# Second attention of a four-layer kernel: the largest-score pass in two row tiles, key preparation on GpSimd, the causal mask partly added by TensorE

## The reference, cut to what matters

```python
def _L1_attn_ref(x, w_attn, w_proj):      # B 8, T 512, D 128, H 16, HEAD_D 8
    qkv = x @ w_attn
    q = qkv[..., :D].reshape(Bv, Tv, H, HEAD_D).transpose(0, 2, 1, 3)
    k = qkv[..., D:D + HEAD_D]
    v = qkv[..., D + HEAD_D:]
    att = jnp.einsum('bhqd,bkd->bhqk', q, k) * scale
    att = jnp.where(causal[None, None, :, :], att, -jnp.inf)
    att = jax.nn.softmax(att, axis=-1)
    y = jnp.einsum('bhqk,bkd->bhqd', att, v)
    ...
    return y @ w_proj
x = x + _L1_attn_ref(_layernorm(x), L1_attn_w_attn, L1_attn_w_proj)
```

## Time and profile before

| what | us |
|---|---|
| median of 3 runs (848.96 to 860.17) | 853.83 |
| the profiled execution | 861.02 |
| its span, first to last instruction | 859.3 |
| third layer's largest-score pass of sequence 0, before turn 0 | 470 to 504 |
| one steady turn (four of them alike) | 41.60 |

### The profile page before, as it was taken

The page is one execution under the profiler, slowest core; times in us unless marked ns, Lnnn a source line. Parts: engine busy times, 40 slices in busy tenths (PEclk is TensorE's granted clock), DMA queues, the critical chain, the costliest instruction groups (busy, mean ns, idle before and its releaser), DMA issues. The chain is left out here.

```text
span 859.3 us, 14978 instructions
## 1 busy us (share of the span) xinstructions
PE 681.4 (79%) x4376; PEld 413.4 (48%) x4409; DVE 583.3 (68%) x1923; ACT 349.4 (41%) x748; POOL 328.8 (38%) x430
## 2 busy tenths in 40 slices
PE   1579989984048999999974779898989898898794
PEld 1445666652025788777762224444444444443353
DVE  8378888886921312544357988888889898977373
ACT  0322333304302212222311127666666666666761
POOL 0256656640065636677630003333333332333330
PEclk9999999997558859999995579999999999999996
DMA  9200000000411212222234213020404040300021
GB/s 297 80 1 1 0 1 0 1 1 26 134 40 32 37 19 35 34 40 38 35 77 55 37 22 49 12 57 3 56 4 56 3 57 9 50 4 3 1 62 38
DMA packets 40350, 32.44 MB, mean 38 GB/s; under 512 B 3608, under 2 KB 36936, under 8 KB 40280
## 3 DMA queue, kind: packets, MB, share of 16 engines
q1 hardware_dynamic: 30448, 23.51, 12.6%
q0 software_dynamic: 7840, 6.86, 5.4%
q10 hardware_dynamic: 1992, 1.21, 0.8%
HBM read 13.60 MB, written 8.13 MB: 25 GB/s over the span
## 5 line engine op out<-in xcount | busy, mean ns | idle before, releaser
L1602 ACT ACTIVATE pexp<-wide 128x512 f32<-128x512 f32 (+2 forms) x384 | 183.7, 543 | 118.5 <-PE wide L1791 112.3
L1551 POOL TENSOR_SCALAR_AFFINE_SELECT pexp<-pexp 128x256 f32<-128x256 f32 x256 | 107.3, 422 | 284.1 <-ACT pexp L1602 282.6
L1414 DVE CUSTOM_DVE_ANT_0 masked<-bank,mask_qk 128x384 f32<-128x384 f32 (+3 forms) x356 | 155.2, 480 | 22.0 <-PE bank L1742 20.0
L1791 PE MATMUL wide<-qT,kTe 128*128 128x256 bf16 (+3 forms) x501 | 120.7, 301 | 19.0 <-ACT pexp L1602 8.8
L1070 ACT ACTIVATE hT<-wide,b1T 128x512 f32<-128x512 f32 x64 | 43.5, 687 | 162.8 <-PE wide L1090 134.3
L1742 PE MATMUL bank<-kTm,qT 128*128 128x384 bf16 (+3 forms) x348 | 89.0, 320 | 17.1 <-DVE mx L1414 8.7
L1804 PE MATMUL bank<-pexp,vx 128*32 128x512 f32 (+3 forms) x1024 | 95.5, 445 | 0.8 <-POOL pexp L1551 0.8
L945 POOL DMA_INDIRECT x_dram<-yg,row_u x40 | 63.9, 1596 | 58.0 <-DVE yg L994 49.5
L1414 DVE CUSTOM_DVE_ANT_0 masked<-wide,mask_qk 128x256 f32<-128x256 f32 (+3 forms) x156 | 74.3, 499 | 15.5 <-PE wide L1742 12.9
L938 POOL DMA_INDIRECT x_row<-xln_dram,row_u x64 | 61.8, 965 | 52.8 <-DVE slot_tok L815 33.6
L1099 PE MATMUL bank<-w_sb,hT 128*128 128x128 f32 x512 | 75.4, 292 | 3.2 <-issue 3.2
(11 more groups left out here) (232 smaller groups left out, 1071.8 us busy)
## 6 DMA issues: line engine op xcount, KB each, us to landing
qT<-qp SPq DMA_DIRECT2D x135, 64.0 KB
x_sb<-in_L_attn_x SPq DMA_DIRECT2D x8, 256.0 KB, 6.7
w_sb<-in_L_ffn_w SPq DMA_DIRECT2D x1, 2048.0 KB, 13.1
xln_dram<-rx SPq DMA_DIRECT2D x8, 256.0 KB, 2.3
out_x<-x_sb SPq DMA_DIRECT2D x8, 256.0 KB, 2.3
x_dram<-x_sb SPq DMA_DIRECT2D x5, 256.0 KB, 3.5
x_sb<-x_dram SPq DMA_DIRECT2D x5, 256.0 KB, 3.0
x_row<-xln_dram,row_u POOLq DMA_INDIRECT x64
```

The lines of the kernel that those rows point to most:

```text
L1414: ins = nc.vector.tensor_tensor_reduce(out=masked[:, n % 4, at], in0=bank_of(n)[:, at], in1=mask_qk[:, T - w:T], scale=1.0, scalar=LEAST, ...
L1551: nc.gpsimd.affine_select(out=pexp[:, n % 4, :, 0:P], in_=pexp[:, n % 4, :, 0:P], pattern=[[0, 2], [1, P]], compare_op=ALU.is_ge, fill=0.0 ...
L1602: nc.scalar.activation(pexp[:, (2 * step + h // 2) % 4, h % 2:h % 2 + nh, 0:w], psE[m % 3][:, 0:nh * w].rearrange("p (h t) -> p h t", h=nh ...
L1791: ins = nc.tensor.matmul(psE[m % 3][:, hh * w:(hh + 1) * w], kTe[:, par, j * P:(j + 1) * P], qT[:, b % QB, 4 * qd + h + hh, j * P:T], star ...
```

## The change

- **Row tiles.** `qT` and `kTm` get 15 blocks of 8 rows (120) in place of nine (72). Heads 0 to 7 have their six largest products in rows 0 to 47, heads 8 to 15 in rows 64 to 111, and the other three products further down. The largest-score pass now uses those six products alone, so that a unit of heads 0 to 7 and one of heads 8 to 15 form a pair: their matmuls have 48 rows each, in rows 0 to 63 and 64 to 127 of the array, and go to two banks. The second pass goes on with all nine (rows 0 to 122 with the three for the maximum; the blocks of the other half are zero).
- **Pairs.** Units are issued two at a time, so `PAIRS_IN_STEP` takes the place of `IN_STEP`; the pair waits for both banks and for the query rows of both halves.
- **Mask.** For query tiles 0 and 1 PE adds the mask by four more matmuls of 64 rows per pair (identity against mask, own and other half of the rows), and DVE takes the maxima of the whole bank with one `tensor_reduce`. Tiles 2 and 3 stay as they were.
- **Keys on POOL.** The five operations of the key parts, the key slots (four copies in place of three) and the values' copy move from DVE to POOL, into its order before the zeroings of steps 6, 7 and 2. The DVE copy `kTe` is gone: `kTm` has three buffers and the rows of -1, which POOL writes at the program's start after the constants have come.
- **Zeros.** The start clears 64 rows of half the heads twice, instead of `kTm` and 64 rows of all heads. The constants grow by 256 columns, 128 KB.

```diff
-    QR = PARTS * PARTS * L
+    BLOCKS = 2 * P // 16 - 1
+    QR = BLOCKS * L
+    LARGE = 6 * L
+    ROWS_OF_HALF = (((0, 3, 5), (1, 4, 6), (2, 7, 14)), ((8, 11, 13), (9, 12, 6), (10, 7, 14)))
+    KEYS_IN_BLOCKS = ((0, 0, 2, 0, 3), (1, 0, 2, 3, 5), (1, 0, 1, 7, 8), (2, 0, 2, 5, 7))
...
-        IN_STEP = (4, 3, 2, 2, 1, 2, 2, 2, 5, 4, 3, 3, 2, 4, 2, 3)
-        AHEAD = sum(IN_STEP[SHIFT_STEP:])
+        PAIRS_IN_STEP = (2, 2, 1, 1, 1, 1, 1, 0, 2, 2, 2, 1, 1, 1, 2, 2)
+        AHEAD = 2 * sum(PAIRS_IN_STEP[SHIFT_STEP:])
...
+                n = 2 * (spot in spots[:PAIRS_IN_STEP[s]])
...
+            part, g0, ng, lo, hi = KEYS_IN_BLOCKS[n]
+            return ops(kx3[:, :, g0:g0 + ng, lo % 8:lo % 8 + hi - lo, :],
+                       kp[:, part].unsqueeze(2).unsqueeze(2).broadcast_to([P, NT, ng, hi - lo, L]))
...
+        def pool_k_parts(pool, b):
+            pool.wait_ge(q_kv.sem, q_kv.at(b, 1))
+            pool.wait_ge(q_kx.sem, q_kx.at(b, 0))
+            split(pool, nc.gpsimd, q_kpart, b, kv2[:, :, 0:L], k_rest[:, :, :], [kp[:, n] for n in range(PARTS)])
...
-        def dve_kTe(dve, b, par):
...
+                if k in MASKED_BY_PE:
+                    nc.vector.tensor_reduce(mx[:, k, h:h + nh], bank_of(n)[:, :].rearrange("p (h t) -> p h t", h=nh),
+                                            AX.X, ALU.max).then_inc(q_mx.sem, 1)
+                    continue
...
+        def pool_turn(pool, b, middle=True, front=True):
+            for s in range(STEPS):
+                if middle and s == V_STEP:
+                    pool_v(pool, b + 1, 1 - b % 2)
+                if front and s == K_SPLIT_STEP:
+                    pool_k_parts(pool, b + 2)
+                if front and s == SLOT_STEP:
+                    pool_k_slots(pool, b + 2)
+                pool_causal(pool, b, 2 * s)
+                pool_causal(pool, b, 2 * s + 1)
...
-        def pe_max_unit(pe, b, n, place):
+        def pe_max_pair(pe, b, n, places):
+
             k, h, nh = max_units[n]
-            pe.wait_ge(q_row[h // 8].sem, q_row[h // 8].at(b, PARTS * PARTS))
+            for half in range(2):
+                pe.wait_ge(q_row[half].sem, q_row[half].at(b, PARTS * PARTS))
             pe.wait_ge(q_kTm.sem, q_kTm.at(b, 1))
             w = P * (k + 1)
             for hh in range(nh):
-                ins = nc.tensor.matmul(place[:, hh * w:(hh + 1) * w], qT[:, b % QB, h + hh, k * P:(k + 1) * P],
-                                       kTm[:, b % 2, 0:w], start=True, stop=True)
-            ins.then_inc(q_smp.sem, 1)
+                for half, place in enumerate(places):
+                    rows = slice(64 * half, 64 * half + LARGE)
+                    ins = nc.tensor.matmul(place[:, hh * w:(hh + 1) * w],
+                                           qT[rows, b % QB, 8 * half + h + hh, k * P:(k + 1) * P],
+                                           kTm[rows, b % QB, 0:w],
+                                           start=hh == 0 or k not in MASKED_BY_PE, stop=k not in MASKED_BY_PE)
+                    if hh == nh - 1 and k not in MASKED_BY_PE:
+                        ins.then_inc(q_smp.sem, 1)
+            if k in MASKED_BY_PE:
+                for whose in ("own", "other"):
+                    for half, place in enumerate(places):
+                        rows = slice(64 * half, 64 * half + 64)
+                        ins = nc.tensor.matmul(place[:, :].rearrange("p (h t) -> p h t", h=nh)[:, :, w - P:w],
+                                               by_mask["ident_" + whose][rows, :],
+                                               by_mask["causal_" + whose][rows, :].unsqueeze(1).broadcast_to([64, nh, P]),
+                                               start=False, stop=whose == "other")
+                        if whose == "other":
+                            ins.then_inc(q_smp.sem, 1)
...
-            nc.vector.memset(kTm[64:P, :, :], 0.0).then_inc(s_zero.sem, 1)
-            nc.vector.memset(qT[64:P, :, :, :], 0.0).then_inc(s_zero.sem, 1)
+            nc.vector.memset(qT[64:P, :, 0:HEADS // 2, :], 0.0).then_inc(s_zero.sem, 1)
+            nc.vector.memset(qT[0:64, :, HEADS // 2:HEADS, :], 0.0).then_inc(s_zero.sem, 1)
```

More of the change, by code:

```diff
@@ L1367, in split @@
                 if n:
-                    dve.wait_ge(sig.sem, sig.at(b, n))
+                    engine.wait_ge(sig.sem, sig.at(b, n))
                 if n % 2 == 0:
-                    nc.vector.tensor_copy(part, whole if n == 0 else rest).then_inc(sig.sem, 1)
+                    on.tensor_copy(part, whole if n == 0 else rest).then_inc(sig.sem, 1)
                 else:
[L1372 to L1377, removed]
@@ L1395, in dve_kTe, with dve_q_parts @@
-        def dve_kTe(dve, b, par):
[L1396 to L1399, removed]
+                    on.tensor_tensor(rest, whole if n == 1 else rest, part, ALU.subtract).then_inc(sig.sem, 1)
+        def dve_q_parts(dve, b, ops):
+            split(dve, nc.vector, q_qpart, b, psA[:, :], q_rest[:, :], [qp[:, n] for n in range(PARTS)], ops)
@@ L1424, in dve_shift @@
             dve.wait_ge(q_mTp.sem, q_mTp.at(b, 0))
[L1425 removed]
+            split(dve, nc.vector, q_mpart, b, mx[:, :, :], mx[:, :, :], [mp[:, :, n, :] for n in range(PARTS)])
         def dve_shift_T(dve, b):
@@ L1553, in pool_causal @@
                                     channel_multiplier=-1).then_inc(q_pc.sem, 1)
-        def mqa_pool(pool):
-            with nc.gpsimd.Fori(0, B) as b:
-                for n in range(NX):
-                    pool_causal(pool, b, n)
+        def pool_turn(pool, b, middle=True, front=True):
[8 more added lines that the diff above has]
+                pool_causal(pool, b, 2 * s + 1)
+        def mqa_pool(pool):
+            pool_k_parts(pool, 0)
+            pool_k_slots(pool, 0)
+            pool.wait_ge(q_init.sem, q_init.total(4))
+            pool_v(pool, 0, 0)
+            pool_k_parts(pool, 1)
+            pool_k_slots(pool, 1)
+            for b in range(B):
+                pool_turn(pool, b, middle=b + 1 < B, front=b + 2 < B)
         def act_xln(act, b, tiles=range(NT)):
@@ L1680, in q_rows @@
                 queue.wait_ge(q_qpart.sem, q_qpart.at(b, 2 * n + 1))
-                for j in range(PARTS):
-                    row = (n * PARTS + j) * L
+                for block in ROWS_OF_HALF[half][n]:
+                    row = block * L
                     queue.dma_start(qT[row:row + L, b % QB, 8 * half:8 * half + 8, :],
@@ L1986, in constants @@
         "seqmask": ((n[:, None] % 64) // 8) == np.arange(8)[None, :],
-        "shift_rows": np.where((n >= 72) & (n < 75), -1.0, 0.0)[:, None],
+        "shift_rows": np.where((n >= 120) & (n < 123), -1.0, 0.0)[:, None],
     }
+    causal = parts["causal_qk"]
+    for name, a in (("ident_own", np.eye(P)), ("ident_other", np.roll(np.eye(P), P // 2, axis=0)),
+                    ("causal_own", causal), ("causal_other", np.roll(causal, P // 2, axis=0))):
+        halves = np.ascontiguousarray(a, np.float32).view(np.uint32) >> 16
+        parts[name] = (halves[:, 0::2] | (halves[:, 1::2] << 16)).astype(np.uint32).view(np.float32)
     layout, at = {}, 0
```

107 lines of the change are left out of this document (47 added, 60 removed).

## The result

The kernel after took 876.15 us (875.04 to 878.82, four runs), the kernel before 851.81 in the same session: a ratio of 1.0274, 95% interval 1.0194 to 1.0353. Repeated with the experiments, on a chip where the kernel before takes 838 us, it was 865.75 us and 1.0334 (1.0317 to 1.0352). The forecast was 852 us, range 831 to 870: wrong in sign and outside the range.

A forecast was written before the change was run, and what follows sets the result against it. No engine was held full; DVE and PE hand PSUM banks back and forth, each late at times. Turns with POOL -2.9, before turn 0 +1.3, start -0.5: -2.1 from the 853.8 us median gives 852, range 831 to 870.

The forecast's parts named there:

- DVE, maxima and keys: DVE in a turn: 1.5 us saved on maxima, 1.7 on keys, together 3.2 us (2.0 to 3.6).
- PE, streams and shape changes: PE in a turn: 2.6 us of streams saved, 37 shape changes at 0.10 us cost 3.7, net 1.1 us more.
- Rivals 2 and 3: PE in the turns: shape changes make it the bound, 874 to 882, chance 0.14; row tiles don't stream together, 888, 0.04.
- rival 2: PE becomes the bound through 37 shape changes a turn at 0.20 us each; 874 to 882 us, chance 0.14.
- POOL: POOL's key work at steps 6 and 7 delays the values: 0.75 us per turn (0 to 1.5), six turns, +4.5.
- What a turn gains: Steady turn: DVE's -3.2 and PE's +1.1 both halved, -1.05 us; seven turns -7.4, with POOL's +4.5 -2.9.
- Before turn 0: Pass ahead of turn 0: first pair waits for both halves' query rows, 4 us later; together +1.3 us (-1 to +4).
- given back: 3.5: Pass before turn 0: 1.5 us of maxima, 1.4 + 0.6 of sequence 1's keys and DVE's wait for them regained.
- Rival 4: The pass before turn 0 loses more, +4 us with nothing in the turns: 857 us, chance 0.06.
- Turn 0: First of the seven turns' worth of maxima (turns 0 to 6), counted at the same -1.05 us each.
- The program's start: DVE's clearing at the start: same 12288 words, without the 0.48 us for `kTm`; -0.5 us (-3 if the gap was real).
- I am wrong in the middle if the schedule of units ... set the turn: Closing caveat on the turns: which bank comes free when is beyond the engines' sums; no size or chance given.

The follow-up runs named there:

- e2: Kernel after with the turns' key parts, key slots and values' copy back on DVE at their old places; ratio 1.0262 to the kernel before.
- f1: Kernel before with keys and values' copy on POOL behind the zeroings, three key buffers, no `kTe`; single units in old order, mask on DVE; ratio 0.9934.
- e4: Kernel after without row tiles: maxima products over rows 0 to 119, mask products over 128 rows, unit after unit; ratio 1.0262.
- f2: f1 with PE adding the mask of tiles 0 and 1 over the whole array; ratio 0.9971, steady turn 41.4 us.
- h4: Kernel before in spread single units, keys and mask on DVE, with the pairs' numbers per step and without the `kTe` copy; ratio 1.0012.
- f3: Kernel before with the pairs' order, whole array, mask and turns' keys on DVE, start's keys on POOL, three key buffers, no `kTe`; ratio 1.0205.
- g2: f3 with the old numbering, so both units of a pair are of one half; ratio 1.0108.
- h1: g1 with a step's two units spread over places B and D (then A and C) instead of both at B; ratio 1.0121.
- g1: f3 with units issued one by one, each waiting only for its own bank and its own half's rows; ratio 1.0178.
- e1: Kernel after with DVE's divide ahead of the two maxima where a place has both; ratio 1.0247, steady turn 43.1 us.
- e3: Kernel after with POOL's key parts and slots behind the two zeroings of their step instead of ahead; ratio 1.0247.
- h2: f3 with one pair moved from step 1 to step 7 and one from step 14 to step 13; ratio 1.0299.
- h3: Kernel after with the edits of e1 and e3 and the pairs per step of h2; ratio 1.0074.
- i2: Kernel after, unchanged, run again on the chip of the experiments; ratio 1.0334, attention stage 435.4 us.

## Why the prediction was wrong

- **DVE, maxima and keys:** right in sum, 33.16 busy in the turn, and in the spacing, 0.61. The keys alone were worth 1.0 to 1.3 of busy time (e2, f1), not 1.7.
- **PE, streams and shape changes:** right. Row tiles stream together: 689.12 and 689.12, then 689.34 and 689.34 above, 512 columns each, as the Trainium skill ("TensorE: Matmul & The Clock Gate", Part 3: Packing small matmuls) says. The lines above show 0.10 to 0.11 us a change, and e4's sum fits it. Rivals 2 and 3 were both wrong in their mechanism; that the measured time lies in rival 2's range, 874 to 882, is luck.
- **POOL:** right, 1.02 us of wait; I charged 0.75, taking it away gave 0.4 to 1.1. The five operations took 0.21 to 0.25 us each. The two subtractions among them, with two inputs, took 0.25 where DVE took 0.18 and 0.32 in the steady turn of the kernel before, so the factor of two of the Trainium skill ("GPSIMD Engine Reference", Performance versus the Vector engine) doesn't show at this size.
- **What a turn gains:** this step failed. "Both late about half of the time at the margin, and I halve both" gave -1.05 us, and with POOL -0.3; measured +2.3. Even in the old order halving held only in part: f1's relief of 1.3 on DVE gave 0.9 us, but f2's 1.6 less on DVE and 1.4 more on PE, by halving -0.1, cost 0.7. What the step left out is that the order itself changed. From h4's 41.3 us on, which have the pairs' numbers per step, the runs put on it about 0.6 us for the new numbering (f3 to g2, and h4 to h1), 0.9 for both units at B ahead of the divide (g1 to h1; 0.8 by e1) and 0.1 for the two banks (f3 to g1): 42.9, f3's turn. POOL's place adds 0.4 to 1.1 (e3), which makes 43.3 to 44.0 around the measured 43.9, with nothing left for DVE's 3.2 us: in this order its relief is idle time (2.01 us at a stroke above). That the parts add up so well is not to be relied on, as h2 and h3 show.
- **Before turn 0:** +4.3 (+4.2 in i2), just past the end of -1 to +4. The delay was right in kind and too small: the first maximum came 26.5 us after the stage's start instead of 24.3; 0.8 of that come with the mask products, at 1.2 GHz here (25.7 in f3, without them). Of "given back: 3.5" came 1.9: from the first maximum to turn 0 it took 31.6 us, before 33.5. Over the whole pass DVE was busy 41.10 of 58.16 us, before 46.20 of 53.90, and PE was at 1.2 GHz throughout (0.50). Rival 4, whose price was +4, had this part.
- **Turn 0:** counted like a steady turn. It lost 5.6 to 7.1 us (i2 and the kernel after, which are one kernel) where a steady turn lost 2.3; in h4, with single units, 2.1. The rest stays open.
- **The program's start:** right. DVE's first statistics start at 13.76 us, before at 14.29.
- **"I am wrong in the middle if the schedule of units ... set the turn"** was the true case. It got no price and no chance, and it was to be had: the kernel has `dve_max` ahead of `dve_divide` at place B, the diff makes it two units there instead of one, and the chain y, back transpose, scores, next pair is in the code. Four divides a turn, 0.6 us later each by the 0.61 us of a maximum, bound it at an estimated 2.4 us; 0.8 to 0.9 of it came.

## What to carry to other kernels

When a change regroups work, cost its order too: for each place list what stands behind the grouped operations on their engine, and who waits for that. An engine's sum tells what may be won, only the order tells whether it is. Put the short operation on which another engine waits ahead of the long ones that only fill a buffer; here two moved lines gave 0.5 to 0.8 us a steady turn, in the old order and in the new.

## What the runs showed of the hardware that was new to me

- Row tiles of half the array: two matmuls of 64 rows and 512 columns start at the same hundredth of a microsecond and stream together (689.12 and 689.34 above), which saves 0.21 us a pair; the two changes of shape around a pair, 0.10 us each, take as much. By this sum a pair with one matmul of 512 columns a tile gains nothing.
- The same shift of two pairs cost 1.1 to 1.7 us a turn with keys and mask on DVE (h2) and gained 1.1 to 2.0 with them on POOL and PE and the divide first (h3). Which of the two moved pairs does it was not tried.
